# Four row maxima of a group in one stationary matrix, 32 columns apart

## What is computed

```python
xn = _layernorm(x)
scores = einsum('bsd,de,bte->bst', xn, qk, xn) / sqrt(128)      # causal: -inf above the diagonal
attn = softmax(scores, axis=-1)
attention = einsum('bst,btd,de->bse', attn, xn, ov)
eid = argmax(xn @ centroids.T);  alpha = sigmoid(sum(xn * centroids[eid]))
ffn = onehot(eid) * (relu(xln @ w1[e] + b1[e]) @ w2[e] + b2[e])  # xln: xn normalised again, ln_g, ln_b
out = x + attention + xn + alpha * ffn
```

## Time and profile before

| what | us |
|---|---|
| median of 3 runs | 223.56 |
| lowest and highest run | 223.23, 226.32 |
| span of the profiled execution | 223.1 |
| TensorE busy (products) | 206.3 |
| VectorE busy | 175.5 |
| ScalarE busy | 155.2 |
| GpSimd busy | 154.3 |

### The profile page before, as it was taken

The page is one execution under the profiler, slowest core; times in us unless marked ns, Lnnn a source line. Parts: engine busy times, 40 slices in busy tenths (PEclk is TensorE's granted clock), DMA queues, the critical chain, the costliest instruction groups (busy, mean ns, idle before and its releaser), DMA issues.

```text
span 223.1 us, 6878 instructions
## 1 busy us (share of the span) xinstructions
PE 206.3 (92%) x2428; PEld 159.9 (72%) x2428; DVE 175.5 (79%) x448; ACT 155.2 (70%) x346; POOL 154.3 (69%) x230
## 2 busy tenths in 40 slices
PE   7699776999979999999999999799999999999993
PEld 5544323768856875777766889799999996787773
DVE  6588999899899999999999875556448575535995
ACT  2639989784578899777748755646665658868781
POOL 6173759994259999989999338998999899960000
PEclk9859999999999999999999999999999999999999
DMA  6992003397001111111111696536683111116964
GB/s 167 314 289 64 6 0 94 116 355 232 5 12 39 36 39 39 44 43 40 36 40 36 128 198 160 125 92 141 131 150 92 50 40 37 38 35 172 256 193 141
DMA packets 37601, 23.55 MB, mean 106 GB/s; under 512 B 12472, under 2 KB 34144, under 8 KB 37568
## 3 DMA queue, kind: packets, MB, share of 16 engines
q1 hardware_dynamic: 34960, 18.28, 32.3%
q0 software_dynamic: 2272, 4.69, 6.3%
q10 hardware_dynamic: 336, 0.14, 0.3%
HBM read 11.17 MB, written 9.38 MB: 92 GB/s over the span
## 4 chain that ended last, share of the span: by engine, by line
PE 77%; DVE 11%; ACT 4%; issue 4%; DMA 2%; SPq 1%; DVEq 0%; ACTq 0%
PE psum L1343 6%; PE psum L1300 6%; PE psum L1301 6%; PE psum L1302 6%; PE psum L1351 6%; PE psum L1344 6%; PE psum L1277 5%; PE psum L1460 4%; PE psum L1461 4%; PE psum L1462 4%; PE psum L1434 4%; PE psum L1436 4%; PE psum L1435 4%; PE psum L1260 3%; PE psum L1334 2%
## 5 line engine op out<-in xcount | busy, mean ns | idle before, releaser
L910 DVE TENSOR_TENSOR p_lo<-p_sb,p_hi 128x512 f16<-128x512 f32 (+1 forms) x68 | 42.0, 638 | 12.2 <-ACT p_sb L1050 12.0
L1044 ACT ACTIVATE p_hi<-psum 128x512 f16<-128x512 f32 (+1 forms) x68 | 37.1, 547 | 19.4 <-PE psum L1351 14.2
L1050 ACT ACTIVATE p_sb<-psum 128x512 f32<-128x512 f32 (+1 forms) x80 | 42.5, 539 | 6.8 <-PE psum L1334 6.7
L693 POOL DMA_INDIRECT sorted_y<-xn x39 | 38.1, 977 | 11.6 <-ACT xn L1174 5.5
L1018 DVE SCALAR_TENSOR_TENSOR h_lo<-psum,h_hi 128x512 f16<-128x512 f32 x39 | 26.8, 690 | 21.5 <-ACT h_hi L1166 18.7
L671 POOL MEMSET v_full<- 1x600 f32 x71 | 41.7, 588 | 0.0
L684 POOL DMA_INDIRECT sorted_x<-xr,pos x32 | 33.5, 1047 | 11.9 <-issue 11.4
L1166 ACT ACTIVATE h_hi<-psum 128x512 f16<-128x512 f32 x39 | 23.3, 597 | 21.0 <-PE psum L1436 19.2
L1343 PE MATMUL psum<-v_hi,p_hi 128*128 128x129 f16 x236 | 32.7, 220 | 1.2 <-DVE x_sb L927 1.2
L896 DVE TENSOR_REDUCE row_max<-psum 128x1 f32<-128x512 f32 x48 | 32.3, 682 | 1.6 <-PE psum L1277 1.1
L1344 PE MATMUL psum<-v_lo,p_hi 128*128 128x128 f16 x236 | 32.6, 219 | 0.0
(11 more groups left out here) (189 smaller groups left out, 528.4 us busy)
## 6 DMA issues: line engine op xcount, KB each, us to landing
w_raw<-in_L_ffn_w SPq DMA_DIRECT2D x16, 256.0 KB, 4.2
sorted_x<-zero SPq DMA_DIRECT2D x3, 780.0 KB, 6.4
xn<-sorted_x SPq DMA_DIRECT2D x8, 260.0 KB, 3.9
x_sb<-in_L_attn_input_data SPq DMA_DIRECT2D x8, 256.0 KB, 5.6
xn<-sorted_y SPq DMA_DIRECT2D x8, 256.0 KB, 4.9
out<-x_sb SPq DMA_DIRECT2D x6, 256.0 KB, 3.3
sorted_y<-xn POOLq DMA_INDIRECT x39
sorted_x<-xr,pos POOLq DMA_INDIRECT x32
```

The lines of the kernel that those rows point to most:

```text
L693: pool.indirect_dma_start(out=sorted_y[:, :], out_offset=bass.IndirectOffsetOnAxis(ap=tokens, axis=0), in_=xs[:, t % SLOTS, 0:P], in_offse ...
L910: v.tensor_tensor(p_lo[:, u, off:GW], p_sb[:, u, off:GW], p_hi[:, u, off:GW], ALU.subtract).then_inc(s_plo, 1)
L1044: a.activation(p_hi[:, u, off:GW], bank[SCORE[n % R]][:, off:GW], ACT.Exp, scale=SCALE).then_inc(s_exph, 1)
L1050: a.activation(p_sb[:, u, off:GW], bank[SCORE[n % R]][:, off:GW], ACT.Exp, scale=SCALE).then_inc(s_exp, 1)
```

## The change

max_col shrinks from 4 x 128 to 4 x 32 columns. The column of maxima of query tile i now stands at column 32 i of a single stationary matrix of 128 columns. One product with minus16 turns all four: the row of tile i comes out in partition 32 i of the bank, in columns 0 to 127, where before all four rows stood in partition 0, side by side in 512 columns. ScalarE therefore copies four rows of 128 instead of one of 512; the semaphore is raised by the last of them. The list ORDER and all waits stay.

```diff
-        max_col = sb("max_col", [P, GT, P], F16)
+        max_col = sb("max_col", [P, GT, P // GT], F16)
...
                     a.wait_ge(s_negT, nth["SH", b, g] + 1)
                     a.wait_ge(s_qlo, k + 1)
-                    a.activation(qT_hi[0:1, k * GW:(k + 1) * GW], bank[bank_of["SH", b, g]][0:1, :], ACT.Copy,
-                                 bias=SHIFT, scale=1.0 / W_SCALE).then_inc(s_shift, 1)
+                    for i in range(GT):
+                        turned = bank[bank_of["SH", b, g]][i * (P // GT):i * (P // GT) + 1, 0:P]
+                        ins = a.activation(qT_hi[0:1, k * GW + i * P:k * GW + (i + 1) * P], turned, ACT.Copy,
+                                           bias=SHIFT, scale=1.0 / W_SCALE)
+                    ins.then_inc(s_shift, 1)
...
                 pe.wait_ge(s_rm, nth["RM", job[1], job[2]] + 1)
-                for i in range(GT):
-                    m = mm(at[:, i * P:(i + 1) * P], max_col[:, i, :], minus16[:], start=True, stop=True)
-                m.then_inc(s_negT, 1)
+                mm(at[:, 0:P], flat(max_col[:]), minus16[:], start=True, stop=True).then_inc(s_negT, 1)
```

## The result

The changed kernel took 225.13 us (median of 22 runs, 223.88 to 228.0), the kernel before beside it 224.25 us (22 runs, 222.11 to 226.32): ratio 1.0055, 95% interval 1.0031 to 1.0078. Two more comparisons gave 1.002 (0.9995 to 1.0045) and 1.0051 (1.0024 to 1.0079). The forecast was a gain of 0.68 us and 222.9 us; what came was a loss of about 0.9 us, and 225.13 lies outside the range. The ratios leave out runs of a slower state, so 1.0055 is not the quotient of the two medians, and the profiled execution of the change, with a span of 225.5 us, a time of 227.29 us and a mean granted clock of 0.967, is one of those.

A forecast was written before the change was run, and what follows sets the result against it. The prediction took TensorE to bound the kernel from about 65.4 us on; 0.35 us (three turns before 126 us) + 0.33 (two after) = 0.68 off 223.56 gave 222.9 us, range 222.1 to 224.3.

The forecast's parts named there:

- The products removed: TensorE's turns: three of four products dropped, 0.165 us per group, 0.83 us over the five later groups.
- One copy becomes four: ScalarE's copy in each group: four copies 0.16 us apart, +0.18 us per group, between -0.24 and +0.6.
- The three early groups: First three turns: nothing gained on TensorE; ScalarE's copy starts up to 0.16 us sooner, about offsetting its loss.
- slower: the copies do not overlap: Rival on ScalarE's copies: at 0.26 us each, 1.7 us lost against 0.68 gained, 224.6 us; chance 0.15.
- The slip at 167 us: h_hi behind the copy at 166.43: 0.05 us late, just hidden; 0.43 us late if copies do not overlap.
- What VectorE takes back: Before 126 us: TensorE running ahead may meet VectorE; at most 0.46 us of gain arrives, 0.35 taken.
- The entry: Expert stage's start, 126.19 us: GpSimd's last transfer unmoved, first transposed load has 0.4 us or more room for 0.35.

The follow-up runs named there:

- apart_only: The kernel before, four products kept, but in all eight groups four copies, each row read from its own partition (0, 32, 64, 96): ratio 0.9998.
- b_same: The kernel before, run again unchanged: ratio 0.9992 to the kernel before.
- a_same: The changed kernel, run again unchanged: ratio 1.002 to the kernel before.
- a_again: The changed kernel, run once more unchanged in a later set: ratio 1.0051 to the kernel before.
- early_only: The kernel before with the change made for the first three groups only: ratio 1.0067.
- reads_32: The changed kernel with all four copies of a group reading partition 32: ratio 1.0029 to the kernel before.
- a_pause480: The changed kernel with GpSimd's pause between transfers shortened from 600 elements to 480: ratio 1.0091 to the kernel before.
- a_advance: The changed kernel with GpSimd's first pause shortened from 600 elements to 440: ratio 0.9966 to the kernel before, 0.9982 when repeated.
- product_only: The changed kernel's one product, but one 1x512 copy reading the first tile's row four times: ratio 0.9999 to the kernel before.

## Why the prediction was wrong, point by point

- **The products removed: right.** 0.16 us at the fourth turn, 0.29 between fifth and sixth (4.28 for 4.57 us) and 0.08 between seventh and eighth (28.14 for 28.22) are in the traces, 0.5 us of the 0.83.
- **One copy becomes four: the price was wrong.** It took 0.16 us start to start from two copies that both read from partition 0 on the earlier trace rows. Measured 0.28, and ScalarE is held 1.12 us instead of 0.48: +0.64 us per group for +0.18, past its upper bound of +0.6. "Because the number of columns is the same" overlooked what was not the same, the partition read. The prediction's estimate of 0.80 us for four, from the Trainium skill (ScalarE: Activation LUTs, What ACT_TABLE_LOAD costs), was nearer than the row, and also too low: measured 1.12.
- **The three early groups: wrong for the first.** It set what ScalarE gains by the earlier start against what it loses, so nothing. The first step is 6.76 us for 6.27, about 0.5 us lost, in all traces with these copies; the second step does not win it back (18.7 to 18.9 us in the change for 18.7 before, and 18.0 both in apart_only and in b_same).
- **The rival "slower: the copies do not overlap": its condition came true, its account did not.** It names 0.20 us per copy as the point from which it decides, and its 224.6 lies near what came. But apart_only has exactly these copies and its median loses nothing (the interval allows up to 0.6 us), so most of the 1.7 us it adds up are not there; its trace shows about 0.5 of them, at the first turn. The slip at 167 us was 0.51 us where it took 0.43, and it was made up.
- **What VectorE takes back: wrong question.** It looked for places where TensorE would run into VectorE, and found room. It did not ask what VectorE, running earlier, would run into.
- **The entry: this is the step that failed.** "GpSimd's last transfer, which TensorE's gain does not move": it moved from 119.55 to 122.19 us, 2.6 us, of which only 0.13 was there at the fifth turn. The 0.4 us of room were reckoned for the load alone. The subtraction held by GpSimd's L735 has to end 1.98 us ahead of HI.0 and ended 2.30 us ahead of it in the kernel before, so it had 0.3; in the change and its repeats the entry came 1.1 to 1.6 us later behind the fifth turn, with TensorE standing 1.0 to 1.2 us for p_lo.
- **The clock: not foreseen.** It gave the clock no term. Over all some 360 executions of the experiments the time falls by 0.88 us per 0.01 of the run's mean granted clock. In the comparison of a_same the change stands at 0.9898 and the kernel before at 0.9894, and the change trails by 0.62 us on the mean (standard error 0.22); in that of a_again they stand at 0.9871 and 0.9922, and it trails by 1.07 us (0.31). By the slope the clock goes with none of the first and some 0.4 us of the second. What sets the dips is open: the stretch near 31 to 36 us is in each of the three traces of the unaltered change, and in early_only, reads_32 and a_pause480, but in none of apart_only or a_advance, whose first turn waits as long.

What stays open besides: how often each kernel takes either course at the entry, and so how much of the loss in the medians is made there; this weight is argued, not shown. One trace shows one execution; b_same shows that the kernel before can take the bad one too, and product_only was on it in its trace with a median ratio of 0.9999. The traced execution of b_same took 224.38 us, 1.1 us above the median of its own 12 runs, so there the bad course was not the usual one. Likewise the first three turns took 24.07 in one trace of before and 24.99 in another, with no cause found. And the loss of early_only, whose entry is good (27.88): by the slope its mean clock, 0.9837 for 0.9922, goes with some 0.7 of the 1.2 us of its mean, and the 0.5 us left are as much as its first step is longer (6.75 us for 6.27). That sum is an estimate; no run separates the two.

## What to carry over

Where an engine's chain of work and VectorE's hold each other up, gaining time on a third engine changes who comes first, and a gain of tenths can cost a microsecond; so in the trace list the operations that block each other on both sides of the moved point, with the distance between their starts, before calling a chain unmoved. A price taken from a like row holds only for what is alike: here columns were, the partition was not. And if an edit that saves work loses time, try the pause or the order beside it before dropping it: the change with one pause 160 elements shorter took 222.98 and 222.82 us, beside 223.59 and 223.5 of the kernel before. Then read from the trace what the edit did: this one moved the chain by 0.60 us where 0.16 was meant.

## What the runs showed of the hardware

- ScalarE's copies of one row out of PSUM: four from one partition, 0.72 to 0.74 us (starts 0.16 us apart, also when it is partition 32 and the output partition 0); four from partitions 0, 32, 64 and 96, 1.10 us (0.28 apart); one of 512 columns 0.57.
- A transfer issued by GpSimd (L684) takes 0.96 us alone and up to 1.48 us when VectorE's subtractions of two SBUF operands have just begun; it then ends 0.23 to 0.25 us after them. A transfer that starts 0.27 us ahead of the pair takes 0.96 and does not lengthen the pair's 1.29. A subtraction of 0.69 us takes up to 3.79 beside GpSimd's two-operand operations (L735), ending 0.55 us after them, also where it started 0.98 us before the first of them. A delay of 0.16 or 0.42 us ahead of such a meeting vanishes in it; an advance of 0.16 us grew to 0.60.
